# Macaron block on one core: the value product moved half a period towards its exponentials

## The reference

```python
x = x + 0.5 * ffn(layernorm(x))      # 8 experts, the best 2 weighted, and a gated shared expert
x = x + attention(layernorm(x))      # 16 heads of width 8, causal, ALiBi slopes
x = x + 0.5 * ffn(layernorm(x))
```

## Time and profile before

| what | us |
|---|---|
| median of 3 runs | 318.75 |
| the three runs | 316.54, 320.65, 318.75 |
| profiled execution, its own time | 317.94 |
| its span, first to last instruction | 316.2 |
| first T of group 0 (end of `ffn(0)`) | 97.46 |
| first T of group 1 | 109.05 |
| first T of group 15 | 234.31 |
| last value product of the loop ends | 247.7 |
| PE busy, share of the span | 286.5 (91%) |
| DVE, ACT, POOL busy | 251.3, 175.6, 127.7 |

### The profile page before, as it was taken

One profiled execution on the slowest core, in us unless ns is written; L12 is line 12 of the kernel. 1 busy time (PEld: TensorE's weight loads), 2 busy tenths in 40 slices (PEclk: granted clock), 3 DMA queues, 4 the chain that ended last, 5 costly groups with the idle time before them and its releaser, 6 DMA issues.

```text
span 316.2 us, 7140 instructions
## 1 busy us (share of the span) xinstructions
PE 286.5 (91%) x2328; PEld 185.6 (59%) x2328; DVE 251.3 (79%) x1039; ACT 175.6 (56%) x342; POOL 127.7 (40%) x251
## 2 busy tenths in 40 slices
PE   0889998999998898999799999999999999999994
PEld 0688886977664343334433344333443799989994
DVE  3799898889787787998778989998621698988875
ACT  2423433433555777878578888886888333334330
POOL 1355256306128623575324534666533352420200
PEclk9999999999997599999889999997999999999999
DMA  6910000660022113411113411110000001000011
GB/s 169 244 24 2 0 0 4 224 167 11 3 101 100 42 51 116 151 54 53 51 40 127 140 54 52 54 55 1 4 2 2 0 3 33 2 18 20 1 32 35
DMA packets 20668, 17.73 MB, mean 56 GB/s; under 512 B 2460, under 2 KB 19420, under 8 KB 20572
## 3 DMA queue, kind: packets, MB, share of 16 engines
q1 hardware_dynamic: 19912, 17.05, 18.0%
q10 hardware_dynamic: 720, 0.23, 0.4%
HBM read 9.74 MB, written 7.34 MB: 54 GB/s over the span
## 4 chain that ended last, share of the span: by engine, by line
PE 61%; DVE 14%; POOL 9%; issue 8%; ACT 4%; DMA 2%; SPq 1%; DVEq 0%; POOLq 0%
PE bank L904 16%; PE bank L1033 10%; PE bank L1001 8%; PE bank L839 6%; PE bank L841 5%; PE bank L840 5%; DVE X L699 4%; POOL probs L402 3%; DVE masked_s L767 2%; PE bank L974 2%; DMA X<-in_x 2%; DVE stats L622 2%; PE bank L1043 2%; ACT probs L528 2%; PE bank L1056 2%
## 5 line engine op out<-in xcount | busy, mean ns | idle before, releaser
L767 DVE CUSTOM_DVE_ANT_0 masked_s<-bank,causal_sb 128x512 f32<-128x512 f32 (+3 forms) x256 | 110.0, 486 | 16.0 <-PE bank L974 15.8
L528 ACT ACTIVATE probs<-bank 128x512 f32<-128x512 f32 x160 | 89.7, 602 | 26.0 <-PE bank L1001 25.1
L699 DVE SCALAR_TENSOR_TENSOR X<-bank,coef,X 128x128 f32<-128x128 f32 x272 | 76.2, 342 | 16.2 <-PE bank L904 13.2
L904 PEld LDWEIGHTS bank<-w_sb,act 128*128 128x128 f32 x512 | 67.3, 192 | 6.6 <-ACT act L451 1.1
L904 PE MATMUL bank<-w_sb,act 128*128 128x128 f32 x512 | 67.7, 275 | 0.6 <-ACT act L451 0.6
L402 POOL TENSOR_SCALAR_AFFINE_SELECT probs<-probs 128x512 f32<-128x512 f32 x64 | 39.8, 635 | 65.5 <-ACT probs L528 65.5
L974 PE MATMUL bank<-KA,QA 54*128 54x512 bf16 (+3 forms) x256 | 59.0, 318 | 4.8 <-DVE smax L767 4.1
L451 ACT ACTIVATE act<-bank 128x512 f32<-128x512 f32 x72 | 41.7, 594 | 37.3 <-PE bank L841 36.7
L1001 PE MATMUL bank<-QA,KA 57*128 57x128 bf16 (+3 forms) x256 | 59.3, 317 | 0.9 <-issue 0.7
L1033 PE MATMUL bank<-probs,VA 128*32 128x256 f32 (+2 forms) x640 | 53.6, 403 | 1.4 <-issue 0.9
L839 PE MATMUL bank<-XH,w_hi 128*128 128x512 f32 x88 | 42.3, 481 | 3.0 <-DVE gated L684 1.8
(11 more groups left out here) (87 smaller groups left out, 334.4 us busy)
## 6 DMA issues: line engine op xcount, KB each, us to landing
qk_scratch<-qk_parts SPq DMA_DIRECT2D x8, 384.0 KB, 2.6
QA<-qk_scratch SPq DMA_DIRECT2D x32, 96.0 KB, 2.2
KA<-qk_scratch SPq DMA_DIRECT2D x32, 96.0 KB, 2.3
qk_scratch<-qk_parts SPq DMA_DIRECT2D x8, 256.0 KB, 2.9
qk_scratch<-qk_parts SPq DMA_DIRECT2D x8, 128.0 KB, 2.8
QA<-smaxT SPq DMA_DIRECT2D x64, 3.0 KB
out_x<-X SPq DMA_DIRECT2D x4, 256.0 KB, 2.3
X<-in_x SPq DMA_DIRECT2D x3, 256.0 KB, 6.1
```

The lines of the kernel that those rows point to most:

```text
L528: nc.scalar.activation(dst, src, ACT.Exp).then_inc(exp_done, 1)
L699: m = nc.vector.scalar_tensor_tensor(X[:, b * NT + t, :], Y_BANK[i % 3][:, t * P:(t + 1) * P], coef[:, j % 2, t, n:n + 1], X[:, b * NT + t ...
L767: r = nc.vector.tensor_tensor_reduce(masked_s[:, u % 4, off:off + n], bank[:, off:off + n], causal_sb[:, S - n:S], 1.0, -3e38, ALU.add, AL ...
L904: m = nc.tensor.matmul(Y_BANK[i % 3][:, r], a, w2_sb[:, n, :], start=True, stop=True)
```

## The change

The five pieces of the value product of group n lie in slots 7 and 8 of period n and in slots 0, 1 and 3 of period n + 1. What follows them moves too: `copy_out(n - 1)` to slot 4, `transpose_out(n - 1)` to slot 6, `normalise(n - 1)` to slot 7, and a batch is done one period earlier (n = 4, 8, 12, 16). `transpose_smax` moves from slot 3 to slot 4 and `copy_smax` from slot 3 to slot 5. `project` moves from slot 4 to 2, `high_qk` from 5 to 3, `rest_qk` from 5 to 4, `middle_qk` from 7 to 6. `values(0)` moves from slot 2 of period 0 to the end of `ffn(0)`, on ScalarE ahead of the load of the Exp table. Of the 20 early units three move from the last two expert steps to earlier ones. The transposes for the first two batches of `ffn(1)` go to slot 2 of periods 14 and 15. The last batch's `transpose_out` and `transpose_ao` leave `ffn(1)` for period 16, and its `output` and `add_attention` move to expert steps 1 and 2.

```diff
-        EARLY_STEPS = {(2, 7): 1, (2, 8): 2, (3, 0): 2, (3, 1): 2, (3, 2): 1, (3, 3): 2, (3, 4): 2, (3, 5): 2,
-                       (3, 6): 2, (3, 7): 2, (3, 8): 2}
+        EARLY_STEPS = {(2, 7): 2, (2, 8): 2, (3, 0): 2, (3, 1): 3, (3, 2): 1, (3, 3): 3, (3, 4): 2, (3, 5): 2,
+                       (3, 6): 2, (3, 7): 1}
-        OUT_SLOT = 7
-        VALUE_SLOTS = ((0, 2), (1, 9))
-        XT_TAIL = ((NGT - 2, 4), (NGT - 1, 3))
+        OUT_SLOT = 6
+        VALUE_SLOTS = {(1, 9): 1}
+        XT_TAIL = ((NGT - 2, 2), (NGT - 1, 2))
-            b, rest = divmod(n - 5, NG)
+            b, rest = divmod(n - 4, NG)
...
@@ block.scalar @@
-                        if n == 3 and j == B:
-                            copy_at(B - 1)
             ffn(0)
+            values(0)
             load_table(1, ACT.Exp)
-                    if i == 3 and 0 <= n + 1 < NGT:
+                    if i == 4 and 0 <= n - 1 < NGT:
+                        copy_out(n - 1)
+                    if i == 5 and 0 <= n + 1 < NGT:
                         copy_smax(n + 1)
-                            if i == 5:
+                            if i == 3:
                                 high_qk(b, k)
-                            if i == 7:
+                            if i == 6:
                                 middle_qk(b, k)
-                if 0 <= n - 1 < NGT:
-                    copy_out(n - 1)
...
@@ block.vector @@
-                        if j == B and n == 0:
-                            normalise(NGT - 1)
-                        if j == B and n == 5:
+                        if j == B and n == 2:
                             add_attention(B - 1)
-                    if i == OUT_SLOT and 0 <= n - 2 < NGT:
-                        normalise(n - 2)
+                    if i == OUT_SLOT + 1 and 0 <= n - 1 < NGT:
+                        normalise(n - 1)
-                        if (b := projected_at(n, 2 + k)) is not None and i == 5:
+                        if (b := projected_at(n, 2 + k)) is not None and i == 4:
                             rest_qk(b, k)
...
@@ block.tensor @@
-                            if n == 0:
-                                transpose_out(NGT - 1)
-                            if n == 2:
-                                transpose_ao(B - 1)
-                            if n == 4:
+                            if n == 1:
                                 output(B - 1)
-            PIECE_SLOTS = (2, 3, 5, 6, 8)
+            EARLY_PIECES, LATE_PIECES = {7: 0, 8: 1}, {0: 2, 1: 3, 3: 4}
             ffn(0)
+            values(0)
-                    if i == 3 and 0 <= n + 1 < NGT:
+                    if i in LATE_PIECES and 0 <= n - 1 < NGT:
+                        weigh_values(n - 1, LATE_PIECES[i])
+                    if i == 4 and 0 <= n + 1 < NGT:
                         transpose_smax(n + 1)
-                    if i == OUT_SLOT and 0 <= n - 2 < NGT:
-                        transpose_out(n - 2)
-                    if i in PIECE_SLOTS and 0 <= n - 1 < NGT:
-                        weigh_values(n - 1, PIECE_SLOTS.index(i))
+                    if i == OUT_SLOT and 0 <= n - 1 < NGT:
+                        transpose_out(n - 1)
+                    if i in EARLY_PIECES and 0 <= n < NGT:
+                        weigh_values(n, EARLY_PIECES[i])
-                    if (b := projected_at(n, 2)) is not None and i == 4:
+                    if (b := projected_at(n, 2)) is not None and i == 2:
                         project(b, 0)
-                    if (b := projected_at(n, 3)) is not None and i == 4:
+                    if (b := projected_at(n, 3)) is not None and i == 2:
                         project(b, 1)
```

More of the change, by code:

```diff
@@ L571, in _ @@
                     if (n, i) in VALUE_SLOTS:
-                        values(VALUE_SLOTS.index((n, i)))
-                    if i == 3 and 0 <= n + 1 < NGT:
+                        values(VALUE_SLOTS[n, i])
+                    if i == 4 and 0 <= n - 1 < NGT:
+                        copy_out(n - 1)
+                    if i == 5 and 0 <= n + 1 < NGT:
                         copy_smax(n + 1)
```

## The result

| | before | after |
|---|---|---|
| median, us | 319.21 (4 runs, 316.54 to 320.65) | 362.12 (4 runs, 360.03 to 362.33) |
| profiled execution; span | 317.94; 316.2 | 361.98; 360.2 |
| first T of group 0 | 97.46 | 100.31 |
| first T of group 1 | 109.05 | 113.56 |
| first T of group 15 | 234.31 | 270.48 |

The ratio is 1.139 (95% interval 1.133 to 1.146; the two medians alone give 1.134). The change makes the kernel slower, as forecast, but by 43 us and not by 16: the time lies above the range. By the first Ts, 4.5 us were lost up to group 1's, 31.7 in periods 1 to 14, and 7.8 behind them.

The account below looks back on a forecast made before the run. The prediction took the row maxima's 4.45 us latency behind copy_smax as the loop's bound. From 317.94 us it added 1.3 (start), 13.6 (periods 1 to 14), 2.4 (clock) and 0 (tail): 335.2, forecast 335, range 320 to 348.

Parts of the forecast that it names:

- What bounds the kernel: Group loop: no period shorter than c + 4.45 us, the latency from copy_smax through four DMAs to the next first T.
- c: Time from a period's first T to its copy_smax; forecast 4.81 us instead of 2.82 in periods with nothing extra.
- the lower bound: Lowest c considered, only ScalarE in line: 3.85 us, giving a period of 8.30.
- Rival 2: copy_smax less late than forecast, c about 4.0 to 4.4: time 323.9 to 329.5 us; chance 0.18.
- Rival 3: Value product really in the way, latency not; c falls to 3.85, time to 312.1 us; chance 0.09.
- `values`, `transpose_xn` and `transpose_ao` at slot 9 fall into TensorE's idle time and cost nothing: Slot 9 extras: hidden in 2.3 us idle at each period's end; without cover about 0.5 to 1 us each.
- `project` ... period 10.6: Projection periods 1, 2, 6 and 7: copy_smax at 6.16 us, each period 10.6, 42.4 for the four.
- I take two again, 2.4 us: Clock term for periods 1 to 14: two falls to half clock, as before, costing 2.4 us together.
- Rival 1: Half clock in every second period, brought by idle time at period ends: 341.9 us; chance 0.26.
- The tail ... I take 0: Period 16: two value pieces leave, -1.14 us; transpose_ao(3) waits about 1.1 for normalise(15); taken as 0.
- Early units ... I take 0.5: End of ffn(0): three moved units put VectorE work ahead of rest_qk, 0 to 2.9 us; taken as 0.5.
- the later copy: Period 0: copy_smax(1) waits for one unit more after the transpose, at half clock, 0.8 us.

Follow-up runs that it names:

- run 2: Kernel before with only the maxima late (transpose_smax at slot 4, copy_smax at 5; projection steps later too), value product unmoved: 327.05 us, ratio 1.025.
- run 7: Value product's move alone: after with maxima, projection, tail transposes, early units and values(0) put back as before: 336.33 us, ratio 1.057.
- run 9: Fillers of run 5 and run 6 added: first kernel to run 4, 344.25 us; second to run 7 (periods 1, 2, 6, 7, 14 without run 5's), 335.89 us.
- run 6: After with 30 filler matmuls into a free bank, in slots 5, 8 and 9 of period 14 alone: 352.13 us, ratio 1.103.
- run 5: After with ten filler matmuls behind slot 5 of periods 0 to 14, written where nobody reads: 349.25 us, ratio 1.092.
- run 4: After with the early units (EARLY_STEPS) placed as in the kernel before: 349.38 us, ratio 1.094.
- run 1: After with transpose_smax and copy_smax back at slot 3, projection steps and tail transposes at their old slots, value product still moved: 342.48 us, ratio 1.074.
- run 8: Run 7 with transpose_out two slots later (slot 8 instead of 6) and normalise at 9: 337.46 us, ratio 1.056.
- run 3: After with two of the four DMAs of the row maxima issued by ScalarE instead of SyncE: 350.52 us, ratio 1.103.

## Why the prediction was right and wrong

**What bounds the kernel: right, for half of the periods.** The 4.45 us behind `copy_smax` hold in after to 0.06 in all plain and `output` periods (3, 5 and 9 to 13) but 4 and 8, which have more at slot 9. In the other seven it is 4.7 to 8.1, and "nearly all of periods 1 to 14" didn't come true; neither did 20 us of waits for the DMAs (13.8) or a first T of group 15 at about 250 (270.48). The loss is where the forecast put it: summed over periods 1 to 14, c rose from 50.3 to 84.7, more than the whole loss, and the time behind `copy_smax` fell from 75.0 to 72.2. But the mean of c was to be 5.47 and is 6.05. Plain periods (9.30 for 9.26), c (4.85 for 4.81) and `output` periods (10.31 to 10.33 for 10.35) came as forecast, and run 2 hit the lower bound (3.86 for 3.85). Rival 2 (c of 4.0 to 4.4) falls with the 4.85. Rival 3 falls with runs 2 and 7: neither late maxima nor the moved value product saves anything.

**Where the 26.8 us between sum (335.2) and profiled execution (361.98) are.** The step that failed most is the price of the clock, 2.4 us for two falls and none in the tail: it was short by 14.8, more than half of what is missing.

- *"`values`, `transpose_xn` and `transpose_ao` at slot 9 fall into TensorE's idle time and cost nothing": wrong for periods 4 and 8.* The idle 2.3 us were taken to lie at the period's end. They lie in two places, since `transpose_out` waits for `copy_smax` (14 times, up to 1.33), and behind it 1.00 is too little cover for `values` and `transpose_ao` with its own wait of 0.8. These two periods take 11.12 and 11.03 with a whole clock (run 9) for 9.26: +3.6. I had asked of each step what it costs, and not of each user of `MISC` who had it before.
- *"`project` ... period 10.6": mis-sized.* c is 7.2 and not 6.16, about half of it because `rest_qk` waits for the maxima of slot 4 and not only for `high_qk` (0.54 of 1.04, run 9). The four periods take 47.4 with 6.8 us of half clock in them (run 9) for 42.4: +5.0.
- *"I take two again, 2.4 us": the largest error of the loop.* Periods 1 to 14 ran over their forecast (138.9) by 18.0; 8.6 of it are the two items above, and 9.4 are left for the clock (period by period, after stands 3.4, 2.6, 0.7, 1.2 and 0.9 above run 9's first kernel in periods 1, 2, 6, 7 and 8, 8.8 in all; the 0.4 of period 14 is in it too, though run 6 shows the same 10.19 without the fall): +7.0 beyond the 2.4. Both factors were too low: there are four falls in periods 1 to 13 and one in 14 and not two, and the four cost 2.2 each by that comparison and not 1.2. That the half clock does this, and isn't only beside it, is shown by runs 5 and 6 and the first kernel of run 9: more matmuls, less time. Run 5, with the start of after, has 7.5 of it. Rival 1 had the mechanism but not the place: the falls of after come at 103.0 in period 0, at 120.1, 137.1, 181.5 and 195.2, one in each projection period, and at 266.8 in period 14. None comes in a plain period with its 1.33 and 1.00 of idle time. The one at 120.1 stands between these two rows of TensorE, and the two windows part there:

```profile
119.52 0.38 PE L980 MATMUL bank<-id_b,smax 128*12 128x128 bf16 x4 [1.59 <-DVE qk_rest L739]
...
121.51 1.08 PE L1036 MATMUL bank<-id_f,OT 128*128 128x128 f32 x4 [0.81 <-ACT smaxT L532]
```

```profile
113.56:120.10 6.54, 4.95 (x49) 1.95 (x51) 4.59 (x14) 4.30 (x8) 1.80 (x6) 1.00 0.23 63
120.10:133.80 13.70, 12.89 (x75) 5.81 (x71) 6.36 (x28) 6.18 (x11) 3.83 (x8) 0.50 0.28 88
```

- *"The tail ... I take 0": right at whole clock (0.4, run 6), wrong as it ran, +7.8.* The clock term was worked out for periods 1 to 14 only. Periods 14 to 16 have no S units to fill TensorE, in either kernel, and in after it fell there once and for long.
- *"Early units ... I take 0.5", and the later copy 0.8: mis-sized, +3.2* (4.5 for 1.3). The upper end, 2.9, was close to what run 4 gives directly, 2.8; but it wasn't VectorE's work that came ahead of `rest_qk`, as I had it, but TensorE held for 2.03 us by two full banks. `rest_qk` came 3.5 later, 2.8 of it by the early units (run 4). The other 1.75 us of the start, for which the forecast had 0.8, stay undivided between `values(0)` and the later copy.

These make 3.6 + 5.0 + 7.0 + 7.8 + 3.2 = 26.6.

**The parts don't add up singly.** From before, the value product with what hangs on it costs 17.6 (run 7), the start a further 6.2 (run 1), the late maxima 19.6: 43.4. In the other order the early units alone give 12.7 back, and late maxima without the rest cost 7.9. Nor can the 17.6 of run 7 be read as a part of after's loss: 14.1 of them lie behind `copy_smax` in periods 1 to 14, where after spends less than before (72.2 us beside 75.0). In a plain period of after the wait of `transpose_out` falls into the 4.45 us of the maxima and lengthens nothing. That an added wait costs more where others have already brought half clock fits these numbers, but no run shows it by itself.

**The Trainium skill** (TensorE: Matmul & The Clock Gate, "Why this matters for your kernels") names a long idle gap as what lets the clock drop. In after the longest idle time ahead of the four falls in projection periods is 1.59 us, and in the 6.5 us ahead of the one at 266.8 it is 1.24. The measurement decides: the clock fell without a long gap. Right ahead of two of the falls TensorE did this:

```profile
263.43:266.83 3.40, 1.86 (x21) 0.84 (x16) 0.69 (x1) 3.27 (x7) 0.64 (x1) 1.00 0.00 0
116.70:120.10 3.40, 1.81 (x25) 0.74 (x26) 2.08 (x7) 2.06 (x4) 0.64 (x1) 0.99 0.02 5
```

Over a longer stretch the busy time doesn't tell them from a plain period: 4.95 of 6.54 us ahead of the fall at 120.1, and 6.96 of 9.30 in a period without one.

## What to carry to other kernels

Before you move a step, list every user of the buffer that it shares, in the order of each engine's stream: a producer moved between another's write and its read can turn free idle time into a wait in the middle, and a wait fixed at one user can appear at the next (runs 7 and 8). A latency of four DMAs for which TensorE already waits up to 0.4 us has no room for a delay of 2 us; ask first how late each step may be. And where idle time appears on TensorE, price it twice, once as time and once for the clock, and look at the stretches where waits come close together (here the projection periods) or work has run out (period 14), behind the loop too.

## What the runs showed of the hardware that was not expected

- The half clock outlasts the idle time ahead of it: 23.9 us at 1.2 GHz with TensorE busy for 23.05 of them (run 6). In periods 1 to 8 of after such stretches lasted 6.8 to 13.7 us. The one around the first T of group 15 lasted 23.9 us in after, 13.7 in run 4 and 6.8 in run 3, although the work there is the same.
- Matmuls that compute nothing can pay for themselves: 10 per period took 12.9 us off the median, 30 in one period 10.0. They were put where TensorE is idle anyway, and even so they gave nothing in run 9's second kernel.
- Four small DMAs issued from one queue take 2.74 us of issue, and 1.1 us of landing behind the last (4.45 with the copy, in six of periods 1 to 14 of after as in four of before, beside different loads); from two queues the whole was as short as 3.3.
